# A graph-network layer in one launch: three buffer distances of the later layers go up by one, and TensorE signals each dense half

## What is computed

```python
xn = layernorm(x)
h = xn
for layer in range(6):                                   # L = 6
    agg = segment_sum(h[src], dst)                       # gather rows, add by destination
    z = (h + agg) @ W1[layer] + b1[layer]
    z = relu(batchnorm(z, g1[layer], be1[layer]))
    z = z @ W2[layer] + b2[layer]
    z = batchnorm(z, g2[layer], be2[layer])
    h = z if layer == 5 else relu(z)
x = x + h + mix(xn)                                      # 8 heads, linear attention without softmax
x = x + ffn(layernorm(x))                                # 8 experts, soft routing
```

## Time and profile before

| | us |
|---|---|
| median of 3 runs | 5272.77 |
| the profiled execution | 5229.82 |
| its span, first to last instruction | 5228.0 |
| front of a later layer (the second of five) | 30.7 |
| middle of a later layer (five of them) | 415.2 to 422.5 |
| tail of a later layer (the second) | 95.9 |
| feed-forward network at the end | about 925 |

### The profile page before, as it was taken

One profiled execution on the slowest core, in us unless ns is written; L12 is line 12 of the kernel. 1 busy time (PEld: TensorE's weight loads), 2 busy tenths in 40 slices (PEclk: granted clock), 3 DMA queues, 4 the chain that ended last, 5 costly groups with the idle time before them and its releaser, 6 DMA issues.

```text
span 5228.0 us, 69828 instructions
## 1 busy us (share of the span) xinstructions
PE 4635.8 (89%) x19111; PEld 3326.3 (64%) x19111; DVE 3077.3 (59%) x7552; ACT 3090.9 (59%) x4248; POOL 2980.1 (57%) x3415
## 2 busy tenths in 40 slices
PE   4777899989887899888997998888898899999999
PEld 3555578667764677557775677646776576666665
DVE  6666666455555565545555455555555556666666
ACT  4555533367665676557675667656675435555555
POOL 5565566136662566626665266634666227877776
PEclk8999999999999999999998999989999989999999
DMA  6334454044432554334442354425443410000000
GB/s 208 109 123 130 132 165 144 27 158 152 143 117 68 160 155 145 102 105 145 151 137 85 119 154 152 128 57 166 149 146 114 150 37 8 8 8 8 8 8 8
DMA packets 197182, 560.41 MB, mean 107 GB/s; under 512 B 44306, under 2 KB 63228, under 8 KB 196668
## 3 DMA queue, kind: packets, MB, share of 16 engines
q0 software_dynamic: 109728, 299.78, 20.3%
q1 hardware_dynamic: 79676, 227.39, 12.2%
q10 hardware_dynamic: 7392, 28.90, 1.4%
HBM read 481.66 MB, written 74.24 MB: 106 GB/s over the span
## 4 chain that ended last, share of the span: by engine, by line
PE 54%; DVE 11%; another core or an unknown queue 11%; ACT 10%; issue 9%; POOL 3%; DMA 1%; DVEq 1%; ACTq 0%; POOLq 0%; SPq 0%
PE bank L1021 17%; PE bank L1204 10%; PE bank L1213 6%; PE bank L1104 5%; PE bank L926 4%; PE bank L923 3%; PE bank L969 3%; ACT bank L1286 3%; PE bank L1050 3%; ACT Gsp L1282 2%; ACT Ac L1300 2%; DVE Gsp L1558 2%; DVE onehot L1568 2%; DVE Z L1682 2%
## 5 line engine op out<-in xcount | busy, mean ns | idle before, releaser
L755 POOL DMA_INDIRECT G<-y_table,idx x1416 | 1376.6, 972 | 1335.4 <-DMA y_table<-BIG 512.2
L1021 PE MATMUL bank<-Ac,Ych 128*128 128x512 f32 x7644 | 1909.1, 402 | 166.7 <-issue 86.4
L1021 PEld LDWEIGHTS bank<-Ac,Ych 128*128 128x128 f32 x7644 | 1471.4, 194 | 544.7 <-issue 143.8
L1300 ACT CAST Ac<-BIG 128x2048 fp32r<-128x2048 uint8 (+1 forms) x546 | 916.4, 1688 | 735.7 <-remote 520.2
L755 POOL DMA_INDIRECT BIG<-y_table,idx x870 | 829.1, 953 | 492.2 <-issue 249.5
L1568 DVE TENSOR_SCALAR onehot<-iota,rel 128x128 fp32r<-128x128 f32 x2290 | 513.0, 298 | 696.0 <-remote 550.1
L1558 DVE TENSOR_TENSOR Gsp<-bank,Gsp 128x512 fp32r<-128x512 f32 x875 | 564.1, 685 | 362.6 <-ACT bank L1286 246.1
L2047 DVE TENSOR_TENSOR G<-G,bank 128x448 f32<-128x448 f32 x784 | 462.0, 619 | 215.4 <-ACT G L1464 114.2
L926 PE MATMUL bank<-Gsp,onehot 128*128 128x512 f32 x1750 | 518.7, 414 | 69.9 <-issue 34.2
L1682 DVE TENSOR_TENSOR Z<-Z,bank 128x512 f32 x546 | 373.8, 685 | 207.3 <-PE bank L1021 85.1
L1469 ACT ACTIVATE G<-G,fsh,fsc 128x448 f32<-128x448 f32 x448 | 333.9, 757 | 250.7 <-DVE G L2047 245.1
(11 more groups left out here) (229 smaller groups left out, 5785.5 us busy)
## 6 DMA issues: line engine op xcount, KB each, us to landing
BIG<-adjacency SPq DMA_DIRECT2D x273, 448.0 KB
BIG<-y_table SPq DMA_DIRECT2D x27, 896.0 KB
G<-y_table,idx POOLq DMA_INDIRECT x1416
y_table<-BIG SPq DMA_DIRECT2D x25, 896.0 KB, 3.8
adjacency<-BIG ACTq DMA_DIRECT2D x7, 3136.0 KB
BIG<-y_table,idx POOLq DMA_INDIRECT x870
BIG<-in_x SPq DMA_DIRECT2D x14, 896.0 KB, 7.4
y_table<-BIG ACTq DMA_DIRECT2D x7, 896.0 KB, 3.6
```

The source lines that it names most:

```text
L755: nc.gpsimd.indirect_dma_start(out=rows[:, j, :], out_offset=None, in_=y_table, in_offset=bass.IndirectOffsetOnAxis(ap=idx[:, t:t + 1], ax ...
L1021: last = mm(bank[2 * (k % 2) + b][:, 0:UW], Ych[pos % 2][:, i, s, b * P:(b + 1) * P], Ac[x_ % NAC][:, i - CA * h, :], start=(i == 0 and s ...
L1300: nc.scalar.copy(Ac[x_ % NAC][:, 0:t1 - t0, :], Land[k % NL][:, t0:t1, :]).then_inc(s_ac, 1)
```

## The change

- `RQ` goes from 4 to 3: three places of `Gsp`, but the raw rows get three places of their own, outside `Gsp`. The gather of quad `n` now waits for ScalarE and VectorE to be done with the rows of quad `n - 3` (`s_gh`), not for TensorE. `quad_high` waits for quad `n - 3` instead of, through the gather, quad `n - 4`. The last quad skips the copy to PSUM. (It is still made for the other quads.)
- `OH` = 3 places of one-hots: those of quad `n + 1` wait for quad `n - 2`.
- `NACL` = 4 places of cast halves in the later layers: the cast of half `x` waits for half `x - 4`. The fourth place lies in the row buffer of the first chunk, so from then on two row buffers serve the row loads, and chunk 3 of the rows goes to a place `Rx` of its own.
- Every dense half counts up `s_dn` at its last matmul.
- The rest of the first chunk's first four tiles (`first_low_terms`) is made by GpSimd; VectorE makes that of three tiles.
- The two `bn_aggr` of a batch norm move between the statistics of the last part, and the statistics of one W1 part move from step 89 to step 90.

The core of the diff:

```diff
-    RQ, RQ0 = 4, 4
+    RQ, RQ0, OH = 3, 4, 3
-    NAC = 3
+    NAC, NACL = 3, 4
+        Acx = f32r_at("Acx", [P, CT - CA, UW], BIG_AT + RB_AT + (NC - NRB) % NRB * RB_BYTES)
+        Rx = at(0, RB_BYTES).rearrange("p (t f) -> p t f", f=D)
-        raw = [places[q // 2].rearrange("p (q j k f) -> p q j k f", q=2, j=GJ, k=2)[:, q % 2, :, 1, :] for q in range(RQ)]
+        raw = [at(QUAD_BYTES + q * RAW_BYTES, RAW_BYTES).rearrange("p (j f) -> p j f", j=GJ) for q in range(RQ)]
+        def casts(l):
+            return NAC if first_layer(l) else NACL
+        def cast_place(l, x_):
+            return Acx if x_ % casts(l) == NAC else Ac[x_ % casts(l)]
         def dense_done(l, x_):
             if first_layer(l):
                 return s_dn, x_ + 1
-            if x_ < PRE:
-                return s_dn, 2 * NBLK0 + (l - 1) * PRE + x_ + 1
-            return s_mmq, quads_before(l) + STEP_OF[x_] + 1
+            return s_dn, 2 * blocks_before(l) + x_ + 1
             def gather(l, n):
-                turn = RQ0 if first_layer(l) else RQ
-                if n >= turn:
-                    hold(pool, s_mmq, quads_before(l) + n - turn + 1)
+                if first_layer(l):
+                    if n >= RQ0:
+                        hold(pool, s_mmq, n - RQ0 + 1)
+                elif n >= RQ:
+                    hold(pool, s_gh, (l - 1) * N1 + n - RQ + 1)
+            def first_low_terms(l):
+                hold(pool, s_sh, l * NC + 1)
+                nc.gpsimd.tensor_tensor(Ych[0][:, 0:CA, 1, :], Rb[row_buffer(0)][:, 0:CA, :],
+                                        Ych[0][:, 0:CA, 0, :].bitcast(fp32), ALU.subtract).then_inc(s_slp, 1)
             def cast_half(l, x_):
-                if x_ >= NAC:
-                    act.wait_ge(*dense_done(l, x_ - NAC))
+                if x_ >= casts(l):
+                    act.wait_ge(*dense_done(l, x_ - casts(l)))
+                elif x_ == NAC:
+                    act.wait_ge(s_yd[row_buffer(0)], stored(l, CHUNKS[0]))
+                    act.wait_ge(s_slp, l)
+                    act.wait_ge(s_sl, l * NC + 1)
             def one_hots(l, n):
-                if n >= 2:
-                    dve.wait_ge(s_mmq, quads_before(l) + n - 1)
+                if n >= OH:
+                    dve.wait_ge(s_mmq, quads_before(l) + n - OH + 1)
             def bank_stats(k, h, n, there, value, l, second):
                 for b in range(FB):
                     dve.wait_ge(there, value + b + 1)
                     V.bn_stats(bst[:, b, k, :], z1_bank(h, b)[:, 0:n]).then_inc(s_bst, 1)
+                    hold(dve, s_bst, (l * (W1_PARTS + HALVES) + W1_PARTS + second * HALVES - 1) * FB + b + 1)
+                    V.bn_aggr(bmv[:, b, :], bst[:, b, 0:parts, :].rearrange("p a s -> p (a s)")).then_inc(s_bn, 1)
```

More of the change, by code:

```diff
@@ L391, in gps_layer, with row_buffer, row_place @@
         CHUNKS = [4, 5, 6, 0, 1, 2, 3]
-        def row_buffer(pos):
-            return CHUNKS[pos % NRB] % NRB
+        def row_buffer(pos, l=0):
+            if first_layer(l) or pos < NRB:
+                return CHUNKS[pos % NRB] % NRB
+            return CHUNKS[1 + (pos - 1) % 2] % NRB
+        def row_place(c):
+            return (Rx, s_yx) if c == NRB else (Rb[c % NRB], s_yd[c % NRB])
         def stored(l, c):
-            first, last = c % NRB == 0, (NC - 1) % NRB == c % NRB
-            uses = len(range(c % NRB, NC, NRB)) + first + last
-            return ((l - 1) * uses + c // NRB + 1 + first + (c == NC - 1)) * LANES
+            chunks = [k for k in range(NC) if k != NRB and k % NRB == c % NRB]
+            parts = lambda k: 1 + (k == 0) + (k == NC - 1)
+            return ((l - 1) * sum(map(parts, chunks)) + sum(parts(k) for k in chunks if k <= c)) * LANES
         def loaded(l, pos):
-            i = row_buffer(pos)
+            i = row_buffer(pos, l)
             first = [p for p in range(NC) if row_buffer(p) == i]
@@ L1536, in copy_rows @@
             def copy_rows(l, c):
-                if c >= NRB:
-                    dve.wait_ge(s_yd[c % NRB], stored(l, c - NRB))
+                before = max((k for k in range(c) if k != NRB and k % NRB == c % NRB), default=None)
+                if c != NRB and before is not None:
+                    dve.wait_ge(s_yd[c % NRB], stored(l, before))
                 for m in range(YP):
@@ L1548, in low_terms @@
                 dve.wait_ge(s_sh, l * NC + pos + 1)
-                for i in range(CT):
-                    last = tt(Ych[pos % 2][:, i, 1, :], Rb[row_buffer(pos)][:, i, :],
+                for i in range(0 if first_layer(l) or pos > 0 else CA, CT):
+                    last = tt(Ych[pos % 2][:, i, 1, :], Rb[row_buffer(pos, l)][:, i, :],
                               Ych[pos % 2][:, i, 0, :].bitcast(fp32), ALU.subtract)
@@ L1686, in part_stats, with bank_stats @@
                     V.bn_stats(bst[:, b, k, :], Zt[:, b, n0:min(n1, N)]).then_inc(s_bst, 1)
-            def bank_stats(k, h, n, there, value):
+            def bank_stats(k, h, n, there, value, l, second):
+                parts = (W1_PARTS, HALVES)[second]
                 for b in range(FB):
@@ L1754, in gather_stage @@
                         added += 1
-                    if n > 1 and w1_at(l, n - 2) is not None:
-                        z1_stats(l, w1_at(l, n - 2))
+                    for m in () if n in (0, 1, N1 - 2) else (n - 3, n - 2) if n == N1 - 1 else (n - 2,):
+                        if w1_at(l, m) is not None:
+                            z1_stats(l, w1_at(l, m))
                     if first_layer(l):
@@ L1783, in bn_coefficients @@
             def bn_coefficients(l, second):
-                n, o, parts = 2 * l + second, 3 * second, (W1_PARTS, HALVES)[second]
-                hold(dve, s_bst, (l * (W1_PARTS + HALVES) + W1_PARTS + second * HALVES) * FB)
-                step = steps(s_bn, n * N_BN, N_BN)
-                for b in range(FB):
-                    step(V.bn_aggr(bmv[:, b, :], bst[:, b, 0:parts, :].rearrange("p a s -> p (a s)")))
+                n, o = 2 * l + second, 3 * second
+                hold(dve, s_bn, n * N_BN + FB)
+                step = steps(s_bn, n * N_BN + FB, N_BN - FB)
                 step(tt(bmu[:, :], bmv[:, :, 0], parl[:, o, :], ALU.add))
```

68 lines of the change are left out of this document (41 added, 27 removed).

## The result

The changed kernel takes 5575.7 us (median of 4 runs, 5532.8 to 5578.0) and the kernel before 5272.3 us (median of 4, 5265.1 to 5281.3): a ratio of 1.0555, with a 95% interval of 1.0502 to 1.0609. I had forecast 5130 us with a range of 4985 to 5255. The sign was wrong.

A forecast was written before the change was run, and what follows sets the result against it. TensorE was taken as the bound, with late signals making engines wait for each other. Middle 22, tail 4, front 1, rows 0.6, aggregates 0.6: 28 us a layer, 141 in five, 0.6 in layer 0; scaled 5130 us, range 4985 to 5255.

The forecast's parts named there:

- The held signals: In middles and front: TensorE's signals can come 6 to 7 us late, tending to come when gather runs end.
- Casts, one-hots, add: In a middle: more slack removes 10.4 us of TensorE's idle for the add, 3.9 for low terms and casts.
- my second rival: Whole kernel: the new signals are as late; only 1 to 8 us a layer gained, 5232 to 5268; chance 0.22.
- "Nobody's" 22.1 us: In a middle: of 22.1 us of TensorE's idle time put down to nobody, 4 us would go.
- The low clock: In a middle: the lower granted clock costs 14 us; half, 7 us, would go with the idle time.
- The gathers: In a middle: freed of TensorE, GpSimd hardly pauses, and pauses are when late signals come; 3 us charged.
- The rival on the slower side: In middles: freed gather runs grow, averaging over about 15 us; 22 us a layer lost, 5384 us; chance 0.08.
- Copies at quad n - 3: In later layers: copies waiting for quad n - 3 cost nothing, as ScalarE already waited for about that step.
- Front: Start of a later layer's stage: 1 us gained; up to 3.5 us of idle if the gather run shortens.
- Tail: End of a later layer's stage: gathers end sooner, last signals on time; 4 us gained, between 0 and 12.
- Rows: Before a later layer's front: GpSimd's low terms take 2.4 us; 0.6 us gained, and 0.6 for aggregates.
- The added signals: In five later layers: 460 increments, taken as 0, between nothing and 3 us a layer; 12 by the skill.

The follow-up runs named there:

- gate_back2: The changed kernel, its gathers from the fifth quad on waiting again for TensorE's quad four before; holding chip: 5269.6 us, 1.0001 of the kernel before.
- gathers_alone3: The changed kernel with the old waits for casts, one-hots and adds, gathers still freed; holding chip: 5556.6 us, 1.0559 of the kernel before.
- after_last: The changed kernel itself, run again on a prompt chip: 4642.1 us, 0.9926 of the kernel before.
- plain_pool: The changed kernel with each later-layer gather replaced by GpSimd's plain DMA, no choice by index; prompt chip: 4605.1 us, 0.9849 of the kernel before.
- plain_pool2: The changed kernel with each later-layer gather replaced by GpSimd's plain DMA, no choice by index; holding chip: 4758.2 us, 0.9026 of the kernel before.

## Why the prediction was wrong, point by point

**The held signals** were read rightly from the earlier trace rows, and the kernel before is 11% faster where they don't occur. What I did not draw from it is that a held signal depends on how long a run of gathers has lasted. So the wait that keeps the runs short is worth more than the slack that the other waits get.

**Casts, one-hots, add.** TensorE's waits went as said. Those for the add, the low terms and the casts were 18.8 us of a middle; I left 4.5 of them, and the rows above leave about 3. The one-hots' waits fell from 97.0 to 15.2 us, but VectorE then waited at the group sum and the add instead; I had named such renamed waits as a sign of being wrong. No time was gained: gate_back2, with all of this, is equal to the kernel before within 0.15%. That is my second rival, "the signals as late", for this part of the change.

**"Nobody's" 22.1 us.** I took 4 away; they became 61.8. I had named this as the step most easily wrong, and it was, the other way round.

**The low clock.** I halved its share along with the idle time. The idle time grew, and so did this share: the granted clock is 0.88 to 0.90, and the same matmuls take 29 us longer in the second middle.

**The gathers.** This is the step that failed. I charged 3 us a middle for them; gathers_alone3 puts the price at 290 us in all, 58 a layer. I had only looked at when late signals could pass, not at what ends a pause. Before, the held signal itself set GpSimd free. Now a signal must first let ScalarE cast and copy, 2.1 us in the time-ordered rows, and the pauses went from 2.4 to 4.7 us. Nor did I ask what keeps a run short: the wait for TensorE ended most runs at 12 gathers or fewer, and the wait for ScalarE lets 10.6 in a middle go beyond. The experiments show that the wait makes the difference. How it does, by longer runs, by longer pauses or by both, is read from the traces, and no experiment parts the two.

**The rival on the slower side** had the right place and sign, at a chance of 0.08, and gave 5384 us. By the traces it had much of the mechanism too: GpSimd's runs grow, and TensorE's unnamed idle time with them. Its condition did not hold as written: in the first traces runs are 12.6 to 13.6 us on average, not over 15 (9.5 to 12.2 before). The average was the wrong thing to watch, as it mixes short runs with those of 13 gathers and more, around which most of the unnamed idle time lies. And it left out that the pauses get longer.

**Copies at quad n - 3** cost nothing, as said: gate_back2 has them and loses nothing. **Front**: from the first dense matmul to the first quad 31.6 to 33.7 us for 30.7 to 32.4, no gain. **Tail**: 4 us were forecast; from the end of quad 73 to that of quad 90 it is 94.0 us on average for 92.4, so none. **Rows**: GpSimd's piece takes 2.37 us (2.4 forecast) and is hidden. From a later layer's last quad to the next dense half it is 75.2 us on average for 76.1; 1.2 us were forecast for rows and aggregates together, 0.9 came.

**The added signals** cost nothing, as I had taken it: 235.5 and 235.6 us with and without them, and middles of 358.1 and 358.9. The rule of the Trainium skill, "TensorE: Matmul & The Clock Gate", "The cost: per-tile semaphore tail", which I had weighed, gives an estimate of 2.4 us a layer for 92 increments. The runs show none of it. The page fits its figure to the tiles of a packed matmul, where the increments follow one another closely; here one in 12 or 16 matmuls counts up, and no run tests the page's own case.

## What to carry to other kernels

Before an engine is freed of a wait, ask what will stop it next and what must then happen before it goes on: the wait may have been what kept its runs short. Look at how the lengths of runs and pauses are spread, and not at their average. Idle time that a profile puts down to nobody is the part of a sum that buffers don't reach, and a forecast should price both signs of it. And where the same kernel takes two quite different times on two chips, measure a change on both: this one is 5.6% slower on one and 0.7% faster on the other.

## What the runs showed of the hardware

- On some chips TensorE's signals are held in long runs of gathers by index, and on others not. On the holding ones the kernel before takes 5267 us and on the prompt ones 4675, with gathers of 0.95 us on both. In the first 6 us of a run the median signal of a quad is 0.01 us late; beyond, 90% and more of them are over 0.5 us late, up to 14.4 us in the changed kernel. In after_last it is 0.01 us for every quad of the middles, in a single run of 285 gathers. What sets the two kinds apart I don't know.
- Late in such runs TensorE itself slows down to a matmul every 1.4 to 2.2 us (2056.5 to 2064.9 us in the rows above), without a cause named. In middles with 67 us of idle time and not 39 the granted clock is 0.90 and not 0.97.
- With plain DMAs from GpSimd, of the same bytes, packets and queue, in runs of 2.2 us, no signal was late. The kernel then takes 9.7% less than the kernel before on a holding chip, though without the choice of rows: on such a chip far more time lies in how the rows are fetched than in the distances.
- The opening ahead of layer 0's dense stage, which also gathers by index, ends at 545 to 550 us on prompt chips and at 677 to 701 us on holding ones; with no gather by index left in the later layers it still does (plain_pool 545, plain_pool2 687), which is most of the 153 us between those two.
